# Two fp32 weight differences on GpSimd, held back until VectorE has written a group's one-hot, in the expert stage of a four-layer block

## What is computed

```python
def _L1_ffn_ref(x, Wg, bg, We, be):
    B, S, D, E = (4, 2048, 512, 8)
    probs = jax.nn.softmax(x @ Wg + bg, axis=-1)
    idx = jnp.argmax(probs, axis=-1)
    p = jnp.take_along_axis(probs, idx[..., None], axis=-1)[..., 0]
    e_idx = idx % We.shape[0]
    h = jax.nn.relu(jnp.einsum('bsd,edf->besf', x, We) + be[None, :, None, :])
    onehot = jax.nn.one_hot(e_idx, We.shape[0], dtype=x.dtype)
    out = jnp.einsum('besf,bse->bsf', h, onehot) * p[..., None]
    return out
...
    x = x + _L1_ffn_ref(_layernorm(x, axis=-1), ...)
```

## Time and profile before

| | |
|---|---|
| median of 3 executions | 1549.07 us (1548.41, 1549.07, and one of 5751.63) |
| the profiled execution | 1545.95 us |
| its span, first to last instruction | 1544.2 us |
| busy in the span: TensorE, VectorE, ScalarE, GpSimd | 95%, 78%, 57%, 32% |
| mean granted TensorE clock, share of full speed | 0.981 |
| the expert stage | from about 1276 us to the end |

### The profile page before, as it was taken

How to read it: one execution, slowest core, us unless ns; L and a number is a source line. 1 busy time by engine, 2 the same in 40 slices (tenths; PEclk the granted TensorE clock), 3 DMA queues, 4 the chain that set the end, 5 groups by cost and what they waited for, 6 DMA issues and landing times. The chain is left out here.

```text
span 1544.2 us, 30116 instructions
## 1 busy us (share of the span) xinstructions
PE 1463.7 (95%) x10666; PEld 1080.3 (70%) x10666; DVE 1208.9 (78%) x2372; ACT 880.7 (57%) x2093; POOL 490.6 (32%) x434
## 2 busy tenths in 40 slices
PE   7899999999999999899999989999999978998997
PEld 5677777777777776544443468888888856876885
DVE  5688888897887665688879867888888757787875
ACT  2444444444444443666558647888889865664342
POOL 0122222222222221200004544455454424664333
PEclk9999999999999999999999999999999988999999
DMA  8411111110111101133107510000000007126641
GB/s 300 167 46 44 44 44 44 45 40 14 36 38 41 35 8 76 45 150 150 76 0 320 191 40 3 4 2 3 4 3 3 4 1 281 74 83 199 193 153 60
DMA packets 47807, 118.34 MB, mean 77 GB/s; under 512 B 9422, under 2 KB 15950, under 8 KB 46032
## 3 DMA queue, kind: packets, MB, share of 16 engines
q1 hardware_dynamic: 42016, 100.03, 18.2%
q0 software_dynamic: 5680, 16.85, 2.8%
HBM read 78.90 MB, written 39.80 MB: 77 GB/s over the span
## 5 line engine op out<-in xcount | busy, mean ns | idle before, releaser
L1749 ACT ACTIVATE c_probs<-c_score,c_minus_top 128x128 f32<-128x128 f32 x512 | 183.4, 423 | 1.5 <-DVE c_minus_top L1861 1.5
L1704 POOL TENSOR_TENSOR c_probs<-c_probs,c_recip 128x1024 f32<-128x1024 f32 x64 | 121.6, 1900 | 170.4 <-DVE c_recip L1867 170.4
L696 POOL TENSOR_TENSOR a_attn_lo_parts<-a_attn,a_attn_hi_parts 128x512 fp32r<-128x512 f32 x64 | 80.5, 1293 | 251.7 <-ACT a_attn_hi_parts L758 251.7
L1749 ACT ACTIVATION_READ_ACCUMULATOR c_probs<-c_score,c_minus_top 128x1 f32 x512 | 134.8, 263 | 0.0
L754 ACT COPY a_attn<-a_pv_ps 128x512 f32<-128x512 f32 x64 | 36.9, 577 | 165.7 <-PE a_pv_ps L1042 165.7
L1419 POOL TENSOR_TENSOR xres<-xres,b_delta 128x512 f32<-128x512 f32 x24 | 40.2, 1686 | 217.2 <-DVE b_delta L1476 217.2
L427 PE MATMUL a_bank<-a_x_hi_parts,a_wq_hi 128*128 128x256 f32 x512 | 106.9, 290 | 0.3 <-PEq L442 0.3
L2315 ACT CAST d_xT_hi<-d_turn 128x512 fp32r<-128x512 f32 x71 | 41.7, 587 | 109.5 <-PE d_turn L2559 109.5
L1010 PE MATMUL a_bank<-a_wo_hi,a_attn_hi_parts 128*128 128x512 f32 x256 | 102.8, 402 | 0.4 <-POOL a_attn_lo_parts L696 0.4
L427 PE MATMUL a_bank<-a_x_lo_parts,a_wq_hi 128*128 128x256 f32 x512 | 102.9, 283 | 0.0
L427 PE MATMUL a_bank<-a_x_hi_parts,a_wq_lo 128*128 128x256 f32 x512 | 102.5, 282 | 0.0
(11 more groups left out here) (324 smaller groups left out, 4342.9 us busy)
## 6 DMA issues: line engine op xcount, KB each, us to landing
hidden<-b_hidden SPq DMA_DIRECT2D x5, 2816.0 KB, 8.1
b_hidden<-hidden SPq DMA_DIRECT2D x5, 2816.0 KB, 10.8
xres<-in_x SPq DMA_DIRECT2D x8, 1024.0 KB, 14.3
d_we<-in_we SPq DMA_DIRECT2D x8, 1024.0 KB, 13.6
xres<-in_w_gate_up SPq DMA_DIRECT2D x7, 1024.0 KB, 5.5
d_got<-rows SPq DMA_DIRECT2D x20, 258.0 KB, 2.9
xres<-rows SPq DMA_DIRECT2D x19, 258.0 KB, 2.8
a_rot<-in_rot SPq DMA_DIRECT2D x16, 256.0 KB, 3.0
```

What stands on the lines that cost most here:

```text
L696: nc.gpsimd.tensor_tensor(of_spread(attn_lo, g), of_spread(attn, g), of_spread(attn_hi, g), ALU.subtract).then_inc(attn_lo_ready, 1)
L1704: nc.gpsimd.tensor_tensor(part, part, recip[:, t % 2, heads].unsqueeze(2).to_broadcast([P, HALF, KEYS]), ALU.mult).then_inc(scaled, 1)
L1749: last = nc.scalar.activation(probs[:, t, at, :], score_ps[:, h, g, :], ACT.Exp, bias=minus_top[:, h, g:g + 1], accum_out=total[:, t, at:a ...
```

## The change

Pieces 2 and 3 of expert e no longer wait for the logits of tile 4e+3, but for the one-hot of group e, which VectorE makes from that tile's logits a little later. Pieces 0 and 1 both wait for the logits of tile 4e (piece 1 waited for tile 4e+1's). The order of GpSimd's list stays as it was.

```diff
-                def weights_low(e, k, tile):
+                def weights_low(e, k):
                     pool.wait_ge(we_hi_ready, KB * e + k + 1)
-                    pool.wait_ge(out_full, tile + 1)
+                    if k < 2:
+                        pool.wait_ge(out_full, TPC * e + 1)
+                    else:
+                        pool.wait_ge(hot_ready, e + 1)
                     nc.gpsimd.tensor_tensor(we_lo[:, e, k], we[:, e, k], we_hi[:, e, k], ALU.subtract).then_inc(we_lo_ready, 1)
...
                 for e in range(EXPERTS):
                     for k in range(2):
-                        weights_low(e, k, TPC * e + k)
+                        weights_low(e, k)
                     if e >= 1:
                         scatter_rows(e - 1)
                     for k in range(2, KB):
-                        weights_low(e, k, TPC * e + 3)
+                        weights_low(e, k)
```

## The result

The changed kernel took 1544.49 us in the median of 14 executions, the kernel before 1548.46 us. The ratio on record, which is taken from the executions of both and isn't the quotient of the two medians, is 0.9981, with an interval from 0.9972 to 0.9990, or -2.9 us (-4.3 to -1.5). Measured twice more beside other kernels it came out at 0.9993 (0.9982 to 1.0004) and 1.0000 (0.9990 to 1.0010). The mean of the three is 0.9991, some -1.3 us: by the bound of 2% no change. Whether there is a small gain the timing alone leaves open: two of the three intervals include no difference at all.

What follows compares the result with a forecast made beforehand. TensorE, never idle in ordinary groups, was taken as the bound, VectorE ahead of group 6's ranks; -0.9 - 0.3 - 1.8 + 2.0 = -1.0 us took the median 1549.07 to 1548.1, range 1545.0 to 1551.1.

Steps and rivals of the forecast that it cites:

- VectorE's short instructions are held by a weight difference: VectorE beside GpSimd pairs: a short instruction waits until the running difference ends; one-hot's and 1.62 us instead of 0.17.
- The one-hots: Groups 1 to 5: without the pair beside it the one-hot comes sooner, TensorE regains its wait; -0.9 us, bounds 0 and -1.2.
- The counting: Group 5 to 6, L2430 to L2436: VectorE gets one step further around the unmoved pair; -0.3 us, from 0 to -0.9.
- the table: Tile 27: L2460 and L2462 no longer held once the pair waits for group 6's one-hot; -1.8 us, bounds -1.2 and -2.0.
- The first product: Product 0, fourth block: TensorE waits for expert 7's pieces 2 and 3, now behind group 7's one-hot; +2.0 us, +1.7 to +2.3.
- the bill: Forecast cost in product 0: TensorE's fourth block waits for the later weight difference; +2.0 us, bounds +1.7 and +2.3.
- It passes to the end: Behind product 0: the chains start from TensorE's end there, so the 2.0 us goes through in full.
- Where the pair lands: Moved pair ends ahead of `places`: gap 0.9 us in group 1, half a microsecond elsewhere, about nothing in group 6; cost 0.
- Rival 3: Collision moves to `places`: a reciprocal and a cast held up to 1.3 us; +0.4 us, or 1549.5; chance 0.08.
- The sum: Whole kernel: -0.9 - 0.3 - 1.8 + 2.0 = -1.0 us, giving 1548.1 us; chance 0.70.
- ranks 7 only 1.0 us earlier: Sign in the changed profile: after about 2 us of wait in product 0, group 7's ranks come 1.0 us before 1406.38.

Runs made afterwards that it cites:

- once that was cleared: Change for experts 0 to 6, expert 7 as before, pieces 0 and 1 of expert 6 also waiting for VectorE's counting; against kernel before 0.9954, again 0.9966.
- The table alone: Kernel before with only pieces 2 and 3 of expert 6 held for the one-hot of group 6; ratio 0.9980, -3.1 us.
- Clearing it: Pieces 0 and 1 of expert 6 also wait for the counting's end, on the change with expert 7 as before; against kernel before 0.9954, again 0.9966.
- the bill alone: Kernel before with only pieces 2 and 3 of expert 7 held for the one-hot of group 7; ratio 1.0016, +2.5 us.
- the split and: Kernel before with the one-hot's 128x4 bitwise and written as four 128x1 instructions; ratio 0.9998.
- The kernels without the bill: Change for experts 0 to 6, expert 7 as before: 0.9971; with expert 6's pieces 0 and 1 also waiting for the counting: 0.9954, 0.9966; against kernel before.

## Why the prediction was right

- **VectorE's short instructions are held by a weight difference.** Right, and shown: the one-hot's bitwise and takes 0.17 us in all eight groups with the pair moved, the two instructions are free at the table, and at the counting once that was cleared, and whether one is held depends on its form.
- **The one-hots, -0.9.** Five periods sum to 69.88 us for 70.86 (one of each kernel stands in the earlier trace rows and above): -0.98.
- **The counting, -0.3, and the table, -1.8.** Together 17.98 to 15.77, -2.21. The table alone gave -1.77, which leaves -0.44 for the counting. It went as described, one instruction ahead of the pair. What was mis-sized is the bound: -0.9 was said to be the most that the counting could give back, from TensorE's one visible wait. Clearing it gave 1.61 more: the 1.22 us that TensorE was still idle in that stretch (15.77 less 14.55), 0.54 of it ahead of the ranks of group 6, and 0.4 of its busy time.
- **The first product, +2.0.** As a wait it is right: from the ranks of group 6 to the fourth block 13.73 us became 15.73, +2.00, and 1.97 in the bill alone. As a cost it is too small, since the clock's fall comes on top (below): the bill alone took 2.34 up to the ranks of group 7 and 2.7 to the end.
- **It passes to the end.** Right: nothing to speak of was made good behind it.
- **Where the pair lands.** No instruction of `places` was held in the changed kernel. In groups 0 to 5 the first one starts 0.68 us behind the pair's end (0.9 was forecast for group 1, half a microsecond for the others); behind group 6 the reciprocal starts 0.12 us ahead of it and still takes 0.17. Rival 3 named the reciprocal as one that would be held, which it isn't.
- **The sum, -1.0.** By the stretches -0.98 - 2.21 + 2.00 = -1.2. Measured -2.9, -1.1 and 0.0, with a mean of -1.3. The -1.0 lies outside the first measurement's interval and inside the other two.

The prediction left one thing out: the clock. It priced TensorE's new idle time at its length. In all three profiles of the change, and in the one with the bill alone, the granted clock fell to 1.2 GHz 1.1 to 1.6 us behind the end of the 1.90 us wait. The ranks of group 7 came 0.4 to 0.6 us later than the wait explains (17.13 - 14.53 = 2.60 in the change, not 2.0), with about as much again behind them. The sign "ranks 7 only 1.0 us earlier" failed by this: counted from the ranks of group 0 they came 0.6 us earlier (102.78 for 103.37). The term that was too small is thus the bill, 2.7 to 3.0 for 2.0, and it is in part offset by gains of 3.2 in place of 3.0.

That the sum came out so near the measured mean is therefore partly luck. Where the late part is alike the profiles put the changed kernel's last stage level with that of before (242.7 and 242.65), while the timed executions say -1.3, and -1.7 and -2.0 at equal clock. One explanation would be that the fall in product 0 comes in some executions only. The profiles are three and four executions out of dozens, how often each fall comes in each kernel was not measured, and this stays open. The idle time ahead of group 6's ranks, which the change shortens, can bring a fall as well, as the split and's profile shows.

The kernels without the bill measured more than their stretches give (-4.5 for -3.2, -7.1 and -5.3 for -4.8). The mean clocks account for most of that: the first two ran at a mean clock 0.0018 and 0.0016 higher than the kernel before beside them, and at equal clock they are at -3.2 and -5.1. Where in those executions the clock stood higher isn't recorded; in the profiles most of the difference lies ahead of the groups.

## What to carry to other kernels

When a short VectorE instruction on a critical chain ends at the very moment a GpSimd instruction does, move the GpSimd work behind the chain's signal, for every instruction of the chain and not only the longest. Then look for the one consumer of the moved work that has no slack, here the first product behind the last group, and leave that instance where it was: one exception turned -1.2 us into -3.2 by the stretches, and -1.3 into -4.5 as measured. For effects of a few microseconds in 1545, compare distances between events inside the stage, and repeat the timing: three measurements of one kernel gave -2.9, -1.1 and 0. Look at the mean granted clock beside each time before a difference of a few microseconds is put down to the change.

## What the hardware showed unexpectedly

- A VectorE instruction held by one GpSimd instruction doesn't always get in between it and the next: the and of 1315.28 waited through both halves of its pair (1.62 us), while the counting's instructions took turns with the halves (1.21 each).
- The 128x1 bitwise ands pass beside a weight difference (four in 0.34 us); the 128x4 and, casts of 128x4 and 128x8, and scalar forms of 128x8 and 1x17 don't. A reciprocal of 128x4 passes too (0.17 us inside the pair of 1373.25). The Trainium skill's page "SBUF — State Buffer", section "Who interferes with whom", names the kinds of instruction that can be held (casts and scalar forms in 2-port modes, and two SBUF inputs, like L2460); the runs agree, and here the 128x1 form of the same operation escapes.
- TensorE's clock fell to half for 3.4 us shortly behind 1.9 us of idle time in the midst of dense matmuls (product 0), in four profiles out of four. Behind the 1.8 to 2.1 us some 21 us after the ranks of group 7 it fell in nine out of 12, and behind the 2.4 to 2.5 us ahead of group 6's ranks in one (the split and) out of six. What tells the cases apart was not tried.
